# A transformer block with routed experts on one core: a later routing of the third batch, other orders at the front and at the end, and tiles of four blocks ahead of tiles of three

## The reference

```python
x = x + attn(layernorm(x))      # q, k, v = x @ w.T + b; qp, kp = elu(q) + 1, elu(k) + 1
                                # kv = sum_s kp v;  out = (qp kv) / (qp . sum_s kp + eps) @ o_w.T + o_b
y = layernorm(x)
gates = softmax(y @ gating_w); topk_w, topk_idx = top_k(gates, 2); norm_w = topk_w / sum(topk_w)
position = running count of each expert, over tokens in order; valid = position < 1280
out_e = relu(buf @ w1 + b1) @ w2 + b2           # buf: the rows of expert e
x = x + sum over the two choices of norm_w * out_e[position]   (0 where not valid)
```

## Time and profile before

| | us |
|---|---|
| median of 3 runs | 2043.91 (2041.79 to 2044.57) |
| the profiled execution | 2038.18 |
| its span | 2036.5 |
| PE busy | 1989.5 |
| DVE busy | 907.8 |
| ACT busy | 627.8 |
| POOL busy | 436.6 |

### The profile page before, as it was taken

One profiled execution on the slowest core, in us unless ns is written; L12 is line 12 of the kernel. 1 busy time (PEld: TensorE's weight loads), 2 busy tenths in 40 slices (PEclk: granted clock), 3 DMA queues, 4 the chain that ended last, 5 costly groups with the idle time before them and its releaser, 6 DMA issues.

```text
span 2036.5 us, 29845 instructions
## 1 busy us (share of the span) xinstructions
PE 1989.5 (98%) x10606; PEld 1762.0 (87%) x10607; DVE 907.8 (45%) x1730; ACT 627.8 (31%) x981; POOL 436.6 (21%) x545
## 2 busy tenths in 40 slices
PE   8999999989999989999999999999999999999996
PEld 7889999988889979998998788889988988988995
DVE  5355675657533443345323423453245244334332
ACT  4433333435322422233222322332224223223321
POOL 2012225264621121022112111021021121120221
PEclk9999999999999999999999999999999999999998
DMA  7212212146231431054104402331044043142221
GB/s 182 76 42 73 84 63 82 60 130 197 59 62 29 147 78 21 21 155 98 21 21 119 113 21 52 112 89 21 21 124 108 21 113 106 33 104 94 54 42 21
DMA packets 115407, 156.12 MB, mean 77 GB/s; under 512 B 28560, under 2 KB 61456, under 8 KB 115344
## 3 DMA queue, kind: packets, MB, share of 16 engines
q1 hardware_dynamic: 93744, 112.13, 17.6%
q0 software_dynamic: 21600, 43.16, 11.3%
HBM read 113.16 MB, written 42.10 MB: 76 GB/s over the span
## 4 chain that ended last, share of the span: by engine, by line
PE 90%; POOL 3%; issue 3%; DVE 2%; DMA 1%; ACT 1%; POOLq 0%; SPq 0%; DVEq 0%; ACTq 0%
PE bank L1433 16%; PE bank L1434 16%; PE bank L1435 16%; PE pair_v L1433 7%; PE pair_v L1435 7%; PE pair_v L1434 7%; PE pair_o L1435 5%; PE pair_o L1434 5%; PE pair_o L1433 5%; POOL slot_table L586 2%; PE bank L1441 1%; PE pair_v L1452 1%; PE pair_o L1452 1%; PE bank L1559 1%; PE pair_o L1655 1%
## 5 line engine op out<-in xcount | busy, mean ns | idle before, releaser
L989 DVE CAST h_hi<-h 128x512 fp32r<-128x512 f32 x320 | 140.0, 438 | 847.6 <-ACT h L736 847.6
L571 POOL DMA_INDIRECT out_dram<-ys,tab_s x80 | 128.5, 1606 | 1003.4 <-DVE ys L982 985.1
L1433 PE MATMUL bank<-w_hi,h_hi 128*128 128x512 f32 x752 | 296.2, 394 | 0.0
L1434 PE MATMUL bank<-w_lo,h_hi 128*128 128x512 f32 x752 | 295.0, 392 | 0.0
L1435 PE MATMUL bank<-w_hi,h_lo 128*128 128x512 f32 x752 | 294.8, 392 | 0.0
L736 ACT ACTIVATE h<-bank,b_cur 128x512 f32<-128x512 f32 x160 | 110.0, 688 | 531.6 <-PE bank L1435 531.4
L736 ACT ACTIVATE h<-pair_v,b_cur 128x512 f32<-128x512 f32 x160 | 110.1, 688 | 495.6 <-PE pair_v L1435 495.6
L1433 PE MATMUL bank<-et_hi,w_hi 128*128 128x384 f32 (+1 forms) x640 | 228.3, 357 | 9.0 <-issue 9.0
L1435 PE MATMUL bank<-et_hi,w_lo 128*128 128x384 f32 (+1 forms) x640 | 227.9, 356 | 0.0
L1434 PE MATMUL bank<-et_lo,w_hi 128*128 128x384 f32 (+1 forms) x640 | 227.5, 355 | 0.0
L1435 PE MATMUL pair_v<-et_hi,w_lo 128*128 128x384 f32 (+1 forms) x640 | 227.4, 355 | 0.0
(11 more groups left out here) (259 smaller groups left out, 3553.6 us busy)
## 6 DMA issues: line engine op xcount, KB each, us to landing
w_raw<-L_ffn_w_dram SPq DMA_DIRECT2D x128, 512.0 KB, 3.6
xb<-_attn_hidden_states_dram SPq DMA_DIRECT2D x32, 256.0 KB, 2.7
xr<-_attn_hidden_states_dram SPq DMA_DIRECT2D x32, 256.0 KB, 3.1
out_dram<-x SPq DMA_DIRECT2D x32, 256.0 KB, 3.5
normed<-x1n SPq DMA_DIRECT2D x32, 256.0 KB, 3.7
normed<-zrow SPq DMA_DIRECT2D x1, 2048.0 KB, 7.9
out_dram<-zrow SPq DMA_DIRECT2D x1, 2048.0 KB, 14.4
b_cur<-L_ffn_b_dram SPq DMA_DIRECT2D x8, 256.0 KB, 4.5
```

The source lines that it names most:

```text
L571: nc.gpsimd.indirect_dma_start(out=out, out_offset=bass.IndirectOffsetOnAxis(ap=tab_s[:, h, 0:1].bitcast(I32), axis=0), in_=ys[:, h, :], i ...
L989: ve_.tensor_copy(h_hi[:, mm % 4, :], h32[:, mm % 2, :]).then_inc(h_split_hi, 1)
L1433: mm_(out_, lh, rh, start=(first and c == 0), stop=False, skip_group_check=shared)
L1434: mm_(out_, lh, rl, start=False, stop=False, skip_group_check=shared)
```

## The change

Six edits. (1) The third batch's five routing pieces come one step later, and with them the early transposes of tile 0 one step earlier (41 and 43 for 42 and 44) and the second early split of w1 three steps later. (2) `EARLY_NEXT` is 15. (3) At the front the first half of wv is loaded ahead of tile 1 and split ahead of `xt_hi` on ACT and ahead of tile 1's statistics on DVE; `matrix_lo` of the other three matrices stands behind the statistics of its step. (4) PE's inner loops change places, and the plan's row offsets with them. (5) The second layer goes over the blocks in the order 3, 0, 1, 2, and so do `y_weighted` and `add_rows`. (6) For three-block tiles one signal comes with the first matmul of the last hidden block.

```diff
-        LOGITS, GATE_VALUES, CHOICES, COUNTS, POSITIONS, RECORDS = ((0, 0, 0), (1, 1, 1), (1, 1, 2), (2, 2, 3), (2, 2, 4),
-                                                                     (2, 2, 5))
+        LOGITS, GATE_VALUES, CHOICES, COUNTS, POSITIONS, RECORDS = ((0, 0, 1), (1, 1, 2), (1, 1, 3), (2, 2, 4), (2, 2, 5),
+                                                                     (2, 2, 6))
...
-        EARLY_TURN = {EARLY_TABLE + 5: (0, 1), EARLY_TABLE + 7: (2, 3)}
+        EARLY_TURN = {EARLY_TABLE + 4: (0, 1), EARLY_TABLE + 6: (2, 3)}
...
-        EARLY_W1 = {EARLY_TABLE + 2: 0, EARLY_TABLE + 6: 1}
+        EARLY_W1 = {EARLY_TABLE + 2: 0, EARLY_TABLE + 9: 1}
...
-        EARLY_NEXT = 14
+        EARLY_NEXT = 15
...
+        Y_ORDER = (3, 0, 1, 2)
...
-            load_matrix(0, wv_t)
+            load_half(0, wv_t, 0)
             load_x(1)
+            load_half(0, wv_t, 1)
...
-                for h in range(BT):
-                    pool.wait_ge(y_done, BT * g + h + 1)
+                for i, h in enumerate(Y_ORDER):
+                    pool.wait_ge(y_done, BT * g + i + 1)
...
-                b = batch_at(t, ROUTE + 1)
+                b = routed_at(t - 1, LOGITS)
...
+                if t == MATRIX_STEPS[0]:
+                    matrix_hi(0, 0)
                 v = tile_at(t, TURN_X)
...
-                for h in range(BT):
-                    if h < 2:
-                        dve.wait_ge(y_full, 2 * g + h + 1)
+                for i, h in enumerate(Y_ORDER):
+                    if i < 2:
+                        dve.wait_ge(y_full, 2 * g + i + 1)
...
                 if t == MATRIX_STEPS[0]:
+                    matrix_lo(0, 1)
...
-                for m_ in range(KC):
-                    if t == MATRIX_STEPS[m_]:
-                        matrix_lo(m_)
...
+                if t == MATRIX_STEPS[0] - 1:
+                    matrix_lo(0, 0)
                 v = tile_at(t, STATS)
                 if v is not None:
                     statistics(v)
+                for m_ in range(1, KC):
+                    if t == MATRIX_STEPS[m_]:
+                        matrix_lo(m_, 0)
+                        matrix_lo(m_, 1)
...
-            planning(ve_.tensor_tensor(rows_f[:, 1], jgrid[:], wide_threes, ALU.subtract))
-            planning(ve_.tensor_scalar(rows_f[:, 1], rows_f[:, 1], 0.0, None, ALU.max))
+            wide_fours = fours.unsqueeze(2).to_broadcast([P, E, TPE])
+            planning(ve_.tensor_tensor(rows_f[:, 1], jgrid[:], wide_fours, ALU.min))
...
-                for h in range(blocks):
+                signals = 0
+                for h in Y_ORDER[BT - blocks:]:
                     toks = slice(P * h, P * (h + 1))
+                    idle = y_full if n == MC - 1 and signals == 0 and blocks < BT else None
...
+                with pe.Fori(0, 2) as t:
+                    with pe.If(t < fours):
+                        tile(e, before + t, BT)
                 with pe.Fori(0, TPE) as t:
                     with pe.If(t < threes):
-                        tile(e, before + t, BT - 1)
-                with pe.Fori(0, 2) as t:
-                    with pe.If(t < fours):
-                        tile(e, before + threes + t, BT)
+                        tile(e, before + fours + t, BT - 1)
```

More of the change, by code:

```diff
@@ L689, in _, with matrix_hi @@
         def _(act):
[L690 to L695, removed]
+            def matrix_hi(m, half):
+                act.wait_ge(st_landed[2 * (m % 2) + half], 16 * (m // 2 + 1))
+                nc.scalar.activation(whi[MATRICES[m]][:, 2 * half:2 * half + 2, 0:D], matrix_half(m, half), ACT.Copy) \
+                    .then_inc(st_hi, 1)
             act.sem_inc(h32_done, 2)
@@ L942, in _, with matrix_lo @@
             dve.wait_ge(const_done, 3)
[L944 to L950, removed]
+            def matrix_lo(m, half):
+                two = slice(2 * half, 2 * half + 2)
+                dve.wait_ge(st_hi, 2 * m + half + 1)
+                ve_.tensor_tensor(wlo[MATRICES[m]][:, two, 0:D], matrix_half(m, half),
+                                  whi[MATRICES[m]][:, two, 0:D].bitcast(F32), ALU.subtract).then_inc(st_lo, 1)
             def split_lo(src, dst, hi, done):
@@ L1355, in _ @@
             rows_of = plan_f[:, COUNT, 0:E]
-            fours, extra, threes = plan_f[:, FOURS, 0:E], plan_f[:, EXTRA, 0:E], plan_f[:, THREES, 0:E]
+            fours, extra = plan_f[:, FOURS, 0:E], plan_f[:, EXTRA, 0:E]
             planning(ve_.memset(plan_f[:], 0.0))
@@ L1376, in _ @@
             planning(ve_.scalar_tensor_tensor(out=packed, in0=fours, scalar=12.0, in1=packed, op0=ALU.mult, op1=ALU.add))
-            planning(ve_.scalar_tensor_tensor(out=threes, in0=extra, scalar=1.0, in1=fours, op0=ALU.add,
-                                              op1=ALU.subtract))
-            wide_threes = threes.unsqueeze(2).to_broadcast([P, E, TPE])
-            planning(ve_.tensor_tensor(rows_f[:, 1], jgrid[:], wide_threes, ALU.subtract))
-            planning(ve_.tensor_scalar(rows_f[:, 1], rows_f[:, 1], 0.0, None, ALU.max))
+            wide_fours = fours.unsqueeze(2).to_broadcast([P, E, TPE])
+            planning(ve_.tensor_tensor(rows_f[:, 1], jgrid[:], wide_fours, ALU.min))
             planning(ve_.scalar_tensor_tensor(out=rows_f[:, 0], in0=rows_f[:, 1], scalar=float(P), in1=rows_f[:, 0],
                                               op0=ALU.mult, op1=ALU.add))
-            planning(ve_.tensor_tensor(rows_f[:, 2], jgrid[:], wide_threes, ALU.is_ge))
+            planning(ve_.tensor_tensor(rows_f[:, 2], wide_fours, jgrid[:], ALU.is_gt))
             planning(ve_.scalar_tensor_tensor(out=rows_f[:, 3], in0=rows_f[:, 0], scalar=float(-SLOTS), in1=rows_f[:, 2],
@@ L1424, in _, with product @@
             pe.wait_ge(dconst_done, 3)
-            def product(out_, left, right, n, first=True, last=True, matrix=None, shared=False):
+            def product(out_, left, right, n, first=True, last=True, matrix=None, shared=False, begun=None):
                 for c in range(n):
@@ L1432, in product @@
                     rh, rl = right(c)
-                    mm_(out_, lh, rh, start=(first and c == 0), stop=False, skip_group_check=shared)
+                    ins = mm_(out_, lh, rh, start=(first and c == 0), stop=False, skip_group_check=shared)
+                    if begun is not None and c == 0:
+                        ins.then_inc(begun, 1)
                     mm_(out_, lh, rl, start=False, stop=False, skip_group_check=shared)
@@ L1486, in second_layer @@
                     pe.wait_ge(y_done, BT * g)
-                for h in range(blocks):
+                signals = 0
+                for h in Y_ORDER[BT - blocks:]:
                     toks = slice(P * h, P * (h + 1))
+                    idle = y_full if n == MC - 1 and signals == 0 and blocks < BT else None
                     ins = product(y_bank[h][:], lambda k: (h_hi[:, n % 4, toks], h_lo[:, n % 4, toks]),
-                                  lambda k: (w2_hi[:, n, :], w2_lo[:, n, :]), 1, first=(n == 0), last=(n == MC - 1))
-                    if n == MC - 1 and h < 2:
+                                  lambda k: (w2_hi[:, n, :], w2_lo[:, n, :]), 1, first=(n == 0), last=(n == MC - 1),
+                                  begun=idle)
+                    signals += 1 + (idle is not None)
+                    if n == MC - 1 and signals <= 2:
                         ins.then_inc(y_full, 1)
```

15 lines of the change are left out of this document (9 added, 6 removed).

## The result

| | median us | lowest to highest |
|---|---|---|
| before, 15 runs | 2042.89 | 2041.25 to 2048.01 |
| changed, 15 runs | 2039.53 | 2038.23 to 2041.69 |
| ratio | 0.9981 | 95% interval 0.9973 to 0.9989 |

A forecast was written before the change was run, and what follows sets the result against it. PE bounds the kernel, busy 1989.5 of 2036.5 us, so only idle and slow-clock time can be won. Terms 4.8 + 1.2 + 0.8 + 3.1 - 1.7 + 1.9 = 10.1 us took the 2043.9 median to 2034; range 2029 to 2041.

The forecast's parts named there:

- loss 1.7 us: Loop over experts: new loop order gives 10.6 us of PE idle for 8.95; bounds gain 3, loss 5.
- gain 1.9: Slow matmuls behind PE's long waits: 3.9 us lost before, 1 us each behind two waits after; bounds 0 and 3.9.
- the gather's 1.2: Early transposes' wait for the gather goes with EARLY_NEXT one step later: gain 1.2 us, bounds 0 and 1.2.
- case C: Rival B plus a dearer loop whose gaps cost the clock three times: within 0.2%, 2042 us, chance 0.10.
- rival B: Stall only moves into steps 41 to 46, or PE's slow clock stays: sum about 4.5, 2039.5 us, chance 0.17.
- a clock of 0.5 over more than 8 us in all: Sign of being wrong: PE's granted clock at 0.5 for more than 8 us in all.
- at no cost: Block order, early signal, fewer planning operations, and next weights loaded in a shorter tile cost nothing.
- The stall: Steps 39 to 41: later routing leaves PE idle 3.4 us for 8.2; gain 4.8 us, bounds 1 to 8.2.
- the front: Waits at steps 5 and 8 go, gain 3.1 us, bound below 2; earlier start adds 0.8.
- The start itself: First value product, operands ready 1.2 us earlier, partly at half clock: gain 0.8 us, bounds 0.4 and 3.
- case D: Loop over experts: returns to the head turn cold, 5 us each; all seven give 2069 us, chance 0.05.

The follow-up runs named there:

- Experiment 9: Changed kernel, fours still first, PE's inner loops run exactly as often as they have tiles: 2024.22 us, ratio 0.9925 to the kernel before.
- experiments 3: Changed kernel with PE's three-block loop ahead of the four-block loop again, plan's row offsets with it: 2030.62 us, ratio 0.9956 to the kernel before.
- experiment 5: Kernel before with only the new order of the front (wv in halves, other matrices behind their step's statistics): 2036.44 us, ratio 0.9973.
- experiment 8: Changed kernel with threes first and POOL's four gathers of tile 0 split two and two over steps 38 and 39: 2031.82 us, ratio 0.9961.
- experiment 10: Changed kernel with threes first, EARLY_NEXT 14, old second-layer order and no early signal, leaving routing and front: 2030.08 us, ratio 0.9951.
- experiment 1: The kernel before, unchanged, run and profiled again: 2041.39 us against 2041.12, ratio 1.0004.
- experiment 6: Kernel before with only the later routing of the third batch and its moved early transposes and w1 split: 2035.82 us, ratio 0.9975.
- experiments 2: The changed kernel, unaltered, run and profiled again: 2037.99 us, ratio 0.9986 to the kernel before.
- experiment 7: Changed kernel with threes first and PE's inner loops run exactly as often as they have tiles: 2026.57 us, ratio 0.9935 to the kernel before.

## Why the prediction was wrong

The step that failed is the sum of the loop over experts, "loss 1.7 us", which came at 4 us of idle time and 4.7 to 7 us of the measured time. Two gains were put too high as well: the clock, "gain 1.9", came at 0, and the gather's 1.2 was not there to win. The measured time lies inside the stated range, between the forecast and case C, which had named a dearer loop and gaps that cost the clock. It also lies on rival B's 2039.5, and that is luck: B's stall in steps 42 to 46 did not come (the longest wait there is 0.8 us), though its slow clock stayed. Of the prediction's signs of being wrong one came, a clock of 0.5 over more than 8 us in all: it was 17 us. That sign was badly set, since the kernel before already had over 20 us of it, 3.4 of them at 97 us behind no wait.

**The loop.** The mechanism was right place by place, and the size was not. Forecast were 3.7, 1.8, 1.5, 0.9 and 2.7 us at the entry and ahead of experts 1, 4, 6 and 7, and they came at 4.0, 2.05, 1.29, 0.97 and 2.86. All are a little too small, and at experts 3 and 5, where nothing was forecast, the ledger finds 0.3 each: 2.8 to 3.2 us, not 1.7. The prediction also put at no cost that experts 2, 4, 5 and 6 load and split their next weights in a shorter tile, "as 0 and 1 did before without a wait". That was misread: the kernel before has a wait for `et_lo` in the last tile of both, and the changed one has it in the last tiles of 2, 4, 5 and 6 too, six for two. They are 0.33 us each in the ledger, 1.3 us more. Together the loop has some 4 us more idle time (entry and loop in the ledger, 14.2 for 10.1). The times say 4.7 to 7, and what is above the idle time is not explained. Experiment 9 shows what kind of cost it is: without stepping over iterations the order costs nothing measurable. The cold branch stays in both orders, 3.3 to 3.8 us, and only changes its place.

**The clock.** The prediction took 1 us each for the two first of its three waits, from one wait of 2.36 us that cost nothing and one of 5.65 that cost 2. But waits of 2.8 to 4.1 us mostly have a stretch of 3.4 us or more at 1.2 GHz with them, in 13 of 15 cases over all profiles, 1.5 to 3 us lost each. The wait of 2.35 us ahead of expert 3 has one in four of the seven profiles that show it (experiments 3, 5, 8 and 10), and none in before, experiment 1 and experiment 6. So that it cost nothing was a draw. The loss is 7.9 and 7.6 us in the two profiles of the changed kernel, 5.6 and 7.9 in those of the kernel before: the gain is 0, and the profile that the forecast was made from had lost 2.3 us less than the next execution of the same kernel.

**The gather.** The 1.2 us appear in one of six profiles of kernels with `EARLY_NEXT` at 14, and experiment 10 finds no gain. A wait in one execution was taken for one of the kernel.

**The stall and the front** were right. Forecast was that 3.4 us stay, behind POOL's shift, `x1n`, `residual` and `lgs`; 3.9 to 4.1 stayed in experiments 2, 3, 6, 9 and 10 (2.1 in the changed kernel's first profile, where PE came 3.3 us late itself, 5.4 in experiment 7). Experiment 8 shows POOL's chain as the cause: with two gathers less ahead of it the wait for `lgs` is gone. For the kernel before the wait is 8.9 us in the second execution, so the gain is 5 us for 4.8. The front gives 3.8 to 4.2 us by step 8 in the two pairs of profiles (64.19 to 60.36, 63.37 to 59.17 at the start of the same matmul) for 3.9. The start itself was forecast to give 0.8 of it and is the weaker part. The first value product starts at 11.05 to 11.5 us in the four profiles with the old front and at 10.3 to 11.5 in the nine with the new one, 0.5 us less in the middle. The rest of the lead by 20 us hangs on when the clock rose in that execution.

**The sum again**, from the second profiles of both: 3.5 for the front's waits and 1.0 for its start (the lead at 20 us, 0.5 of it at the first product), 5.3 for the stall and its neighbours, 0.3 for the clock, less 4.1 for the loop, give 6.0 us where the spans differ by 3.9. The missing 2.1 us are within the 2.9 us that the ledger doesn't explain.

**The branches.** All seven returns were warm, 0.209 us at most, with the bodies in the other order too, and case D did not come. The Trainium skill, "Runtime: NRT & Kernel Launch", section Instruction fetch mechanics, would have them cold by its window of two pages; the traces of both kernels speak against that. They agree with it on the one branch whose target had not run yet, 3.3 to 3.8 us in all thirteen profiles; that this time goes into a fetch is not shown.

## What to carry to other kernels

Count a sequencer's steps at every change from one loop to the next, and let loops run as often as they have work: loops with a fixed count and a test in each iteration cost this kernel 4 us in the one order (experiments 3 and 7) and 12 to 14 in the other (2 and 9; 10.6 between their two profiles). Price a wait with what the clock takes behind it: the stall of 8.2 to 9.6 us lost 2 to 3 us of clock in four profiles, and a wait of 3 to 4 us mostly lost 1.5 to 3 as well, so several short waits cost more than a long one. Profile the kernel before twice ahead of a forecast of 0.5%: a wait of 1.2 us was in one execution only, and the time lost to the slow clock differed by 2.3 us. Once a stall is gone, look at what now runs beside what: in experiment 8 a split grew from 1.2 to 3.0 us.

## What was not expected of the hardware

**The clock at the start.** The granted clock first rises to 2.4 GHz at 15.4 us in the first profile of before and at 9.4 in the second, at 10.5 in after, at 15.8 in experiment 5. In experiment 10 it rises at 9.8, falls again at 13.2 and is back at 16.6. Matmuls of the first value product start some 0.22 us apart before it and 0.12 after. The first 36 of these matmuls take 7.2 us in the first profile of before, 6.1 in the second, 7.5 in experiment 5 and 5.7 in after, so executions of one kernel differ by 1 us and more from there on.

**Signals that come late.** In the first profile of after, PE's last product ended at about 424.0 us, but VectorE was released for `ks`, which waits for an earlier one (started at 420.65), only at 425.71. PE idled 3.34 us behind that, and 0.9 us in the same way at 313.7. The row of `ks`, then all waits of this kind in the profile ("remote" as what ended them):

```profile
425.71 0.16 DVE L1057 COPY ks<-pair_v 128x2 f32<-128x2 f32 x1 [2.95 <-remote]
```

```profile
ACT at_hi L705 <- remote: 6.7, 1, 6.7
ACT qe L870 <- remote: 5.8, 1, 5.8
DVE x L1081 <- remote: 3.0, 1, 3.0
DVE ks L1057 <- remote: 3.0, 1, 3.0
DVE kt L1105 <- remote: 1.8, 1, 1.8
```

Neither the second execution of that kernel nor any other here shows such waits at these places. What holds the signals is open, and no experiment was made on it.
